# A two-block decoder on one core: the output norm's broadcast in four 32-row tiles over four banks, the output product and its norm in other banks

## The chip, the cores and the metric

The kernel runs on one core of a Trainium2 chip. The metric is the device time of one execution in microseconds (us); where several runs are compared, their median.

## The reference

The input x is 32 sequences of 128 tokens by 128 channels, with a context of 128 tokens by 96 channels for each. Six sublayers follow one another, each as `x = layernorm(x + sublayer(x))`: in block 0 a gated recurrent and self-attention sublayer, a cross attention, and a quantised two-layer network; in block 1 a gated delta-rule attention, a cross attention with a mask on the queries, and a two-layer network followed by a spike count. The change lies in block 1, at the end of the delta-rule attention and the start of the cross attention:

```
O   = delta rule of 16 heads, 64 channels each, over 128 tokens
O   = O * rsqrt(mean over the head's channels of O^2 + eps) * rms_w
O   = O * g                                   # one gate for each head and token
x1  = layernorm(x + O @ Wo.T + bo)
k,v = ctx @ Wkv.T                             # of the cross attention that follows
q   = x1 @ Wq.T
```

The reciprocal root and the gate are one number for each head and token. Their product, called f, has to be spread over the 64 channels of its head before O is multiplied by it.

## The kernel before, in words

Everything is fp32 but for the quantised network, the biases and the masks. Activations lie with channels on the 128 partitions and tokens along the row. Work goes in three loops: block 0 up to its cross attention, a short loop that finds the largest hidden value for the quantisation, and a third loop, from line 979 on, for the quantised network and block 1. In the third loop two sequences are in flight, called lanes 0 and 1, for 16 rounds: 32 passes of one sequence. Each lane has half of PSUM, four banks of 512 fp32 columns each (`b[0]` to `b[3]`), and its own buffers.

The order of work is written by hand. `CSTAGES` lists the stages of a pass; `CSLOTS` holds for each engine a string of zeros and ones that says whose lane's next stage comes next on it, and each engine issues its instructions in just that order. Engines wait for each other by counting semaphores: a wait on a named step (`dve_did("ON0")`) holds everything behind it on that engine. On TensorE the strings give around the change: for lane 0 `bc`, `ykv`, then lane 1's `cd` (two transposes, L1187 and L1188), then `Wo1`; for lane 1 `bc`, `ykv`, then lane 0's `lna` (a warming matmul L356 and the centring product L1023), then `Wo1`. On VectorE they give for lane 0 `bc`, lane 1's `Mm` (L1562), `ykv`; for lane 1 `bc`, `ykv`. `keep_warm` (L352) issues matmuls whose result nobody reads; `CWARM` says how many 128-column units a stage gets, and 0 means none.

The stages that the change touches, in order:

- `O` (L1264): O lies in banks 0 and 1. ScalarE takes squares of it and copies it to SBUF as `C` (steps `Oc0`, `Oc1`, L1456).
- `norm1`: TensorE averages the squares by head with column tiles of 32 into bank 2 (L1287); VectorE and ScalarE make `f` (L1598), whose last step on ScalarE comes after `Oc1`.
- `bc` (L1289 to L1295): for each pair p of heads one matmul of `f` with a 0/1 matrix `expand[:, p, :]` gives 128 channels by 128 tokens. The rows of `f` that pair p needs lie in rows 32(p//2) to 32(p//2)+31. Before, each matmul reads 64 rows of the array (pairs 0 to 3 the upper half, 4 to 7 the lower), pairs 0 to 3 go to bank 2 and pairs 4 to 7 to bank 3. VectorE then multiplies, four pairs at a time (L1603): ON0 is `D[0:4] = bank 2 * C[0:4]`, ON1 is `D[4:8] = bank 3 * C[4:8]`.
- `ykv` (L1309 to L1313): keys and values of the cross attention from the context, 128 columns each, into bank 1. It waits for `Oc1` and for step `S` on VectorE. VectorE spreads the keys over the heads with a mask (`Kbd`, L436), ScalarE copies the values (L414).
- `Wo1` (L1296 to L1304): the output product, eight matmuls accumulated into bank 2, with the residual's centring (L1303) between the fourth and the fifth. The first four wait for ON0, the second four for ON1.
- `lng`, `lngv` (L1017 to L1038): square on ScalarE (L1035), mean over channels on TensorE into bank 0 (L1029), reciprocal root on ScalarE (L462, L464), and x1 on VectorE (L1520).
- `yq` (L1317) into bank 0, `qT` on VectorE (L440), and the scores `yS0` (L370), which fill all four banks with four matmuls on 32 rows of the array each.

In the profile an fp32 matmul of this kernel shows as two records, a transpose as one.

Of the kernel before, what the change touches and what calls it, by code (L numbers as in the profile page):

```python
# [19 lines left out]
ALU = mybir.AluOpType  # L20
# [3 lines left out]
P = 128  # L24
# [8 lines left out]
DK = 64  # L33
NP = H // 2
# [116 lines left out]
def decoder(nc, a):  # L151
    with ExitStack() as ctx:
# [792 lines left out]
        with nc.Block() as block:  # L945
# [6 lines left out]
            def _(dve):  # L952
                count = [0]

                def link(ins):
# [34 lines left out]
                   "10011100110011100100010001100000110101"),  # L990
        }, TAILS)
        C_LOADS = 4
        CWARM = {"h": 0, "conv": 2, "alpha": 3, "F": 0, "norm1": 0, "bc": 0, "fc": 4, "pj": 0, "yq": 1, "Wo1": 0,
                 "lna": 1, "lnav": 0, "lngv": 1, "lny": 0, "lnyv": 0, "lnf": 0, "lnfv": 1,
                 "y": {"S": 0, "P": 0, "OT": 0, "AT": 0}}
        halves = ((0, DK), (DK, P))

# [18 lines left out]

        def pe_norm(pe, it, s, t, stage):  # L1017
            n, b = lane[s], lane[s].bank
            keep_warm(b[{"lna": 2, "lnf": 2}.get(stage, 0)], CWARM[stage])
            if stage == "lna":  # L1020
                pe.wait_ge(pc.dve[s], pc.DV.before(it))
                pe.wait_ge(pf.dve[s], pf.DV.upto(it, "x3"))
                mm(b[1][:, 0:P], center[:, :], n.xin[:, :], start=True, stop=True).then_inc(pc.pe[s], pc.PE.step(s, "lnac"))  # L1023
            elif stage == "ln" + t:
                pe.wait_ge(pc.dve[s], pc.DV.upto(it, {"y": "ys", "f": "lx"}[t]))
                mm(b[1][:, 0:P], center[:, :], n.x3[:, :], start=True, stop=True).then_inc(pc.pe[s], pc.PE.step(s, f"ln{t}c"))
            else:
                pe.wait_ge(pc.act[s], pc.AC.upto(it, f"ln{t}sq"))
                mm(b[0][:, 0:P], mean[:, :], n.sq[:, :], start=True, stop=True).then_inc(pc.pe[s], pc.PE.step(s, f"ln{t}v"))  # L1029

        def act_norm(act, it, s, t, stage):
            n, b = lane[s], lane[s].bank
            if stage == "ln" + t:
                act.wait_ge(pc.pe[s], pc.PE.upto(it, "Wo1" if t == "g" else f"ln{t}c"))
                act.activation(n.sq[:, :], b[2 if t == "g" else 1][:, 0:P], ACT.Square).then_inc(pc.act[s], pc.AC.step(s, f"ln{t}sq"))  # L1035
            else:
                act.wait_ge(pc.pe[s], pc.PE.upto(it, f"ln{t}v"))
                ln_exp(act, pc, it, s, f"ln{t}l", f"ln{t}r", eps5)  # L1038

        with nc.Block() as block:  # L1040
            @block.sync
# [43 lines left out]
            def _(pe):  # L1085
                def advance(s, it, stage):
# [202 lines left out]
                    if stage == "bc":  # L1289
                        keep_warm(b[3], CWARM["bc"])  # L1290
                        dve_did("f")
                        for p in (0, 4, 1, 5, 2, 6, 3, 7):
                            rows = slice(DK * (p // 4), DK * (p // 4) + DK)
                            last = mm(pair_out(p, 2), expand[rows, p, :], n.f[rows, :], start=True, stop=True)  # L1294
                        last.then_inc(pc.pe[s], pc.PE.step(s, "bc"))  # L1295
                    if stage == "Wo1":  # L1296
                        keep_warm(b[0], CWARM["Wo1"])
                        for p in range(NP):
                            if p % 4 == 0:
                                dve_did(f"ON{p // 4}")  # L1300
                            last = mm(b[2][:, 0:P], w_o1[:, p, :], n.D[:, p, :], start=(p == 0), stop=(p == NP - 1))  # L1301
                            if p == 3:
                                mm(b[2][:, 0:P], center[:, :], n.x3[:, :], start=False, stop=False)  # L1303
                        last.then_inc(pc.pe[s], pc.PE.step(s, "Wo1"))  # L1304
                    if stage == "lngv":
                        pe_norm(pe, it, s, "g", "lngv")
                    if stage[0] == "y" and stage[1:] in ("kv", *ATTENTION_STAGES):
                        def project():
                            if stage == "ykv":  # L1309
                                act_did("Oc1")  # L1310
                                dve_did("S")
                                mm(b[1][:, 0:P], w_ykv[0:CTX, 0, :], n.ctxT[0:CTX, :], start=True, stop=True)
                                mm(b[1][:, P:2 * P], n.ctxT[0:CTX, :], w_ykv[0:CTX, 1, :], start=True, stop=True).then_inc(pc.pe[s], pc.PE.step(s, "ykv"))  # L1313
                            else:
                                keep_warm(b[3], CWARM["yq"])
                                dve_did("lng")
                                mm(b[0][:, 0:P], w_yq[:, :], n.x1[:, :], start=True, stop=True).then_inc(pc.pe[s], pc.PE.step(s, "yq"))  # L1317
                        pe_attention(pe, pc, it, s, "y", project, False, False, stage, CWARM["y"])
# [151 lines left out]
            def _(dve):  # L1470
                def advance(s, it, stage):
# [42 lines left out]
                    elif stage in ("lnav", "lngv", "lnyv", "lnfv"):  # L1514
# [2 lines left out]
                        if t == "f":  # L1517
                            dve.wait_ge(pc.stored[s], 16 * it + FIRST)
                        out = {"a": x, "g": n.x1[:, :], "y": n.x2[:, :], "f": n.xn[:, :]}[t]
                        then(dve.tensor_tensor(out, b[2 if t == "g" else 1][:, 0:P], n.rstd[:, :], ALU.mult), "ln" + t)  # L1520
                        if t == "g":
                            then(dve.tensor_copy(n.qmask[:, :], n.mask_u8[:, :]), "qmask")
                            dve_did("qmask")
# [49 lines left out]
                    elif stage == "V0":  # L1573
                        for c in range(2):
                            pe_did(f"V{c}")
                            then(dve.tensor_tensor(n.cV[:, c, :, :], b[c][:, :].rearrange("p (a e) -> p a e", e=DK),
                                                   n.cds[:, 2 * c, :].unsqueeze(2).broadcast_to([P, NP, DK]), ALU.mult), f"cV{c}")
                    elif stage[0] == "X":
                        k = int(stage[1:])
                        pe_did(stage)  # L1580
                        new, out = (n.PT1, n.PT0)[k % 2][:, 4:8, :, :], b[3][:, :].rearrange("p (a k t) -> p a k t", a=4, k=2)
                        if k == LEVELS - 2:
                            new, out = new[:, :, 1, :], out[:, :, 1, :]
                        then(dve.tensor_copy(new, out), stage)  # L1584
                    elif stage == "A":
                        pe_did("A")
                        for i in range(2):
                            then(dve.tensor_tensor(n.AT[:, i, :, :, :], b[2 + i][:, :].rearrange("p (c a t) -> p c a t", c=2, a=4),
                                                   mask_at[:, :].unsqueeze(1).unsqueeze(1).broadcast_to([P, 2, 4, DK]), ALU.mult), f"AT{i}")
                    elif stage == "S":  # L1590
                        pe_did("S")
                        then(dve.tensor_tensor(by_bank(n.S), solved(2), by_bank(n.Fp[:, :, DK - 1:DK].broadcast_to([P, NP, DK])), ALU.mult), "S")
                    elif stage == "norm1":
                        then(dve.tensor_scalar(n.x3[:, :], x, b_o1[:, 0:1], None, ALU.add), "xs")
                        pe_did("mo")
                        then(dve.scalar_tensor_tensor(n.zs[:, 0:P], n.t2[:, 0:P], 1e-6, b[2][:, 0:P], ALU.mult, ALU.add), "ve")
                        act_did("oR")
                        then(dve.tensor_tensor(n.f[:, :], n.rk[:, :], n.gb[:, 0:P], ALU.mult), "f")  # L1598
                    elif stage == "bc":
                        pe_did("bc")  # L1600
                        for i in range(2):
                            act_did(f"Oc{i}")
                            then(dve.tensor_tensor(n.D[:, 4 * i:4 * i + 4, :], pairs(2 + i), n.C[:, 4 * i:4 * i + 4, :], ALU.mult), f"ON{i}")  # L1603
                    elif stage == "yAT":
                        pe_did("yAT")
                        then(dve.tensor_tensor(n.x3[:, :], b[2][:, 0:P], n.x1[:, :], ALU.add), "ys")
                    elif stage == "fc":
                        act_did("fr")
                        then(dve.tensor_tensor(n.h[:, :], n.h[:, :], n.h[:, :], ALU.mult), "fr2")
                    elif stage == "pj":  # L1610

                        pe_did("pj")
                        y, total = b[0][:, 0:P], n.OT[:, P:2 * P]
                        then(dve.tensor_scalar(total, y, SPIKE_AT[0], None, ALU.is_gt), "ls1")
                        for i in range(1, 5):
                            dve_did(f"ls{i}")
                            then(dve.scalar_tensor_tensor(total, y, SPIKE_AT[i], total, ALU.is_gt, ALU.add), f"ls{i + 1}")  # L1617
                        dve_did("ls5")
                        then(dve.scalar_tensor_tensor(n.x3[:, :], total, 0.2, n.x2[:, :], ALU.mult, ALU.add), "lx")
# [115 lines left out]
```

## Time and profile before

| | |
|---|---|
| median of 3 runs | 2691.66 us (2690.64 to 2695.48) |
| the profiled execution | 2695.88 us, its span 2694.1 us |
| mean granted TensorE clock | 0.977 of 2.4 GHz |
| TensorE matmul busy | 2387.6 us, 89% of the span |
| VectorE, ScalarE, GpSimd busy | 61%, 61%, 8% |
| the third loop | from about 1036 us to the end; its 32 broadcasts start between 1045.4 and 2658.2 us |

Matmuls are pipelined, and in the profile the end of one is modelled, so two that follow each other overlap; distances between starts are the safer measure. The timeline merges like instructions that follow each other into one row: its start, the time from there to the end of the last, and how many records. The bracket at the end of a row is the idle time of the engine before it, and what ended it. PEld is TensorE's weight load, which runs beside its matmuls. Releasers are inferred from semaphore events.

### The profile page before, as it was taken

To read this page: it belongs to the slowest core of one execution; us is meant where nothing else is said; L and a number is where in the kernel's file an instruction comes from. 1 tells how busy PE (TensorE), PEld (TensorE's weight loads), DVE (VectorE), ACT (ScalarE), POOL (GpSimd) and SP (SyncE) were. 2 spreads that over 40 slices of the span, in tenths; PEclk is the share of its full clock that TensorE was granted. 3 is DMA by queue.
4 is the path that set the end of the run, shared out by engine and by line. 5 is a ranking of instruction groups with operands and counts; after the bars stand their busy time and mean duration, and the time that the engine had idled before them with its cause. 6 is when DMAs were issued, how large, how long until landed. Compare 5 with 4: busy or idle time off the path is not lost.

```text
span 2694.1 us, 92105 instructions
## 1 busy us (share of the span) xinstructions
PE 2387.6 (89%) x40926; PEld 1747.2 (65%) x40930; DVE 1656.2 (61%) x3852; ACT 1635.3 (61%) x3852; POOL 206.0 (8%) x174
## 2 busy tenths in 40 slices
PE   3899998999899658999999899999999998999997
PEld 2666666666666427677677677676676676776765
DVE  3667776777677555665656556556656655565564
ACT  2767676767676425656656656566566565566563
POOL 0000000000000001001101110110010011011100
PEclk8999999999999869999999999999999999999998
DMA  3000000000000010000000000000000000000000
GB/s 107 7 8 7 9 8 8 7 9 8 8 7 9 18 37 6 7 9 7 7 6 6 8 8 6 9 7 7 8 7 7 8 7 7 8 7 7 7 6 4
DMA packets 50792, 29.10 MB, mean 11 GB/s; under 512 B 19808, under 2 KB 48672, under 8 KB 50400
## 3 DMA queue, kind: packets, MB, share of 16 engines
q1 hardware_dynamic: 46080, 21.28, 2.8%
q8 instruction: 323, 5.29, 0.8%
q10 hardware_dynamic: 4320, 1.97, 0.3%
q14 instruction: 69, 0.57, 0.1%
HBM read 17.98 MB, written 5.24 MB: 9 GB/s over the span
## 4 chain that ended last, share of the span: by engine, by line
PE 39%; DVE 12%; ACT 11%; issue 2%; DMA 0%; SPq 0%; DVEq 0%
PE bank L1104 5%; PE bank L1171 2%; PE bank L1301 2%; PE bank L356 2%; PE bank L1134 2%; ACT PT L1356 2%; PE bank L1234 2%; ACT zels L1356 2%; DVE zels L447 2%; DVE h L1617 1%; DVE m L445 1%; PE bank L1220 1%; PE bank L1294 1%; PE bank L1144 1%; PE bank L1203 1%
## 5 line engine op out<-in xcount | busy, mean ns | idle before, releaser
L356 PE MATMUL bank<-w_gate,ident 128*128 128x256 f32 (+3 forms) x960 | 342.7, 439 | 15.6 <-DVE mx L860 14.0
L1014 POOL TENSOR_TENSOR PT<-zels,unit 128x512 f32<-128x512 f32 x160 | 203.4, 1271 | 1470.2 <-ACT zels L1356 1283.2
L421 ACT ACTIVATE zels<-zels 128x512 f32<-128x512 f32 x384 | 234.3, 626 | 92.3 <-DVE zels L447 89.9
L445 DVE TENSOR_REDUCE m<-bank 128x4 f32<-128x512 f32 x384 | 262.1, 683 | 22.5 <-PE bank L375 11.7
L447 DVE TENSOR_TENSOR zels<-bank,m 128x512 f32<-128x512 f32 x384 | 265.6, 692 | 13.3
L1356 ACT ACTIVATE zels<-bank 128x512 f32<-128x512 f32 (+1 forms) x256 | 142.6, 573 | 155.9 <-PE bank L1220 79.6
L387 PE MATMUL bank<-ident,zels 128*128 128x128 f32 x1536 | 218.4, 278 | 11.1 <-ACT zels L421 9.5
L1356 ACT ACTIVATE PT<-bank 128x512 f32<-128x512 f32 x256 | 147.8, 598 | 89.6 <-PE bank L1277 48.7
L424 ACT ACTIVATE PT<-bank 128x512 f32<-128x512 f32 x384 | 199.6, 594 | 1.8 <-PE bank L387 1.8
L387 PEld LDWEIGHTS bank<-ident,zels 128*128 128x128 f32 x1536 | 172.7, 142 | 36.5 <-ACT zels L421 21.6
L356 PEld LDWEIGHTS bank<-w_gate,ident 128*128 128x128 f32 x960 | 147.1, 193 | 54.2 <-issue 26.3
L1220 PE MATMUL bank<-zels 64*64 64x64 f32 x5120 | 154.9, 220 | 4.5 <-issue 4.4
L1356 ACT ACTIVATE W<-bank 128x512 f32<-128x512 f32 x192 | 114.1, 594 | 54.1 <-PE bank L1234 27.2
L1218 PE MATMUL bank<-zels 64*64 64x64 f32 x4096 | 135.6, 223 | 10.5 <-DVE zels L1584 7.1
L1220 PEld LDWEIGHTS bank<-zels 64*64 64x64 f32 x5120 | 133.0, 135 | 9.7 <-issue 5.9
L370 PE MATMUL bank<-Kbd,qT 32*128 32x512 f32 x768 | 110.4, 643 | 30.1 <-DVE qT L440 16.9
L1218 PEld LDWEIGHTS bank<-zels 64*64 64x64 f32 x4096 | 113.6, 134 | 35.9 <-issue 28.1
L393 PE MATMUL bank<-PT,V 128*32 128x128 f32 x3072 | 124.0, 280 | 3.3
L462 ACT ACTIVATE rstd<-bank,eps 128x128 f32<-128x128 f32 x224 | 81.4, 363 | 51.9 <-PE bank L1029 46.6
L1584 DVE COPY zels<-bank 128x512 f32<-128x512 f32 (+1 forms) x160 | 100.9, 631 | 13.5 <-PE bank L1220 11.9
L393 PEld LDWEIGHTS bank<-PT,V 128*32 128x32 f32 x3072 | 70.9, 109 | 43.0 <-ACT PT L424 36.1
L1234 PE MATMUL bank<-W,PT 64*64 64x64 f32 x4096 | 89.7, 223 | 4.7 <-issue 4.0
(293 smaller groups left out, 5043.8 us busy)
## 6 DMA issues: line engine op xcount, KB each, us to landing
ctxT<-in_ctxT_dram SPq DMA_DIRECT2D x64, 48.0 KB, 1.8
x_after_cross_attention<-x SPq DMA_DIRECT2D x32, 64.0 KB, 1.6
h<-x_after_cross_attention SPq DMA_DIRECT2D x8, 256.0 KB, 2.8
xin<-x_after_cross_attention SPq DMA_DIRECT2D x32, 64.0 KB, 1.8
out_dram<-xn SPq DMA_DIRECT2D x32, 64.0 KB, 1.6
x<-in_xT_dram ACTq DMA_DIRECT2D x30, 64.0 KB, 1.8
input_integers<-xq SPq DMA_DIRECT2D x8, 128.0 KB, 2.0
xq<-input_integers SPq DMA_DIRECT2D x32, 32.0 KB, 1.8
```

The source lines that it names most:

```text
L356: mm(bank[:, 0:cols], ident[:, :], w_gate[:, :, :].rearrange("p a b -> p (a b)")[:, 0:cols], start=True, stop=True)
L387: last = xp(b[u][:, j * P:(j + 1) * P], n.zels[:, u, j * P:(j + 1) * P], ident[:, :])
L393: last = mm(b[0][32 * j:32 * j + 32, u * P:(u + 1) * P], n.V[:, HU * u + j, :], n.PT[:, u, j * P:(j + 1) * P], start=True, stop=True)
L421: act.activation(n.zels[:, u, :], n.zels[:, u, :], ACT.Exp, scale=ATT_SCALE).then_inc(ph.act[s], ph.AC.step(s, f"{t}P{u}"))
L424: act.activation(n.PT[:, u, :], b[u][:, :], ACT.Copy).then_inc(ph.act[s], ph.AC.step(s, f"{t}PT{u}"))
L445: dve.tensor_reduce(top, scores, AX_X, ALU.max).then_inc(ph.dve[s], ph.DV.step(s, f"{t}max{u}"))
L447: dve.tensor_tensor(n.zels[:, u, :].rearrange("p (h k) -> p h k", h=HU), scores, top.unsqueeze(2).broadcast_to([P, HU, P]), ALU.subtract). ...
L1014: pool.tensor_tensor(n.TI[:, k % 2, :, :], (n.PT0, n.PT1)[k % 2][:, :, 1, :], unit[:, :].unsqueeze(1).broadcast_to([P, NP, DK]), ALU.add)\
L1218: mm(solve_out(p, dst, 2, 0, P), PT[src, p, 1, :], PT[src, p, 0, :], start=True, stop=True)
L1220: last = mm(solve_out(p, dst, 2, DK, P), PT[src, p, 0, :], PT[src, p, 1, :], start=True, stop=True)
L1234: last = mm(solve_out(p, dst, 0), n.TI[src, k % 2, p, :], W[src, p, :], start=True, stop=True)
L1356: ins = act.activation(out, src, func, **how)
```

## The change

The broadcast's eight matmuls read 32 rows each in place of 64. Pairs 2j and 2j+1 go to bank j, columns 0 to 127 and 128 to 255, in the order of the even pairs and then the odd ones, so that four matmuls in turn use four different row tiles and four different banks. ON0 reads banks 0 and 1 (256 columns of each), ON1 banks 2 and 3. Since ON0 now reads bank 1, `ykv` waits for ON0 in place of `Oc1` and `S`. The output product goes to bank 0 in place of 2, its variance to bank 2 in place of 0, with the warming matmul ahead of it; ScalarE and VectorE read them there. The warming call in `Wo1`, of zero units, is gone.

```diff
-        CWARM = {... "yq": 1, "Wo1": 0, "lna": 1, ...
+        CWARM = {... "yq": 1, "lna": 1, ...
...
-            keep_warm(b[{"lna": 2, "lnf": 2}.get(stage, 0)], CWARM[stage])
+            keep_warm(b[{"lna": 2, "lnf": 2, "lngv": 2}.get(stage, 0)], CWARM[stage])
...
-                mm(b[0][:, 0:P], mean[:, :], n.sq[:, :], start=True, stop=True).then_inc(...)
+                mm(b[2 if t == "g" else 0][:, 0:P], mean[:, :], n.sq[:, :], start=True, stop=True).then_inc(...)
...
-                act.activation(n.sq[:, :], b[2 if t == "g" else 1][:, 0:P], ACT.Square).then_inc(...)
+                act.activation(n.sq[:, :], b[0 if t == "g" else 1][:, 0:P], ACT.Square).then_inc(...)
...
-                ln_exp(act, pc, it, s, f"ln{t}l", f"ln{t}r", eps5)
+                ln_exp(act, pc, it, s, f"ln{t}l", f"ln{t}r", eps5, b[2 if t == "g" else 0])
...
-                        for p in (0, 4, 1, 5, 2, 6, 3, 7):
-                            rows = slice(DK * (p // 4), DK * (p // 4) + DK)
-                            last = mm(pair_out(p, 2), expand[rows, p, :], n.f[rows, :], start=True, stop=True)
+                        for odd in range(2):
+                            for j in range(4):
+                                p, rows = 2 * j + odd, slice(QR * j, QR * (j + 1))
+                                last = mm(b[j][:, odd * P:(odd + 1) * P], expand[rows, p, :], n.f[rows, :], start=True, stop=True)
...
-                        keep_warm(b[0], CWARM["Wo1"])
...
-                            last = mm(b[2][:, 0:P], w_o1[:, p, :], n.D[:, p, :], start=(p == 0), stop=(p == NP - 1))
+                            last = mm(b[0][:, 0:P], w_o1[:, p, :], n.D[:, p, :], start=(p == 0), stop=(p == NP - 1))
                             if p == 3:
-                                mm(b[2][:, 0:P], center[:, :], n.x3[:, :], start=False, stop=False)
+                                mm(b[0][:, 0:P], center[:, :], n.x3[:, :], start=False, stop=False)
...
-                                act_did("Oc1")
-                                dve_did("S")
+                                dve_did("ON0")
...
-                        then(dve.tensor_tensor(out, b[2 if t == "g" else 1][:, 0:P], n.rstd[:, :], ALU.mult), "ln" + t)
+                        then(dve.tensor_tensor(out, b[0 if t == "g" else 1][:, 0:P], n.rstd[:, :], ALU.mult), "ln" + t)
...
-                            then(dve.tensor_tensor(n.D[:, 4 * i:4 * i + 4, :], pairs(2 + i), n.C[:, 4 * i:4 * i + 4, :], ALU.mult), f"ON{i}")
+                            four = slice(4 * i, 4 * i + 4)
+                            then(dve.tensor_tensor(n.D[:, four, :].rearrange("p (j a) t -> p j a t", j=2),
+                                                   n.psum[:, 2 * i:2 * i + 2, 0:2 * P].rearrange("p j (a t) -> p j a t", a=2),
+                                                   n.C[:, four, :].rearrange("p (j a) t -> p j a t", j=2), ALU.mult), f"ON{i}")
```

## Rows read from the trace of the kernel before

**Rows 1.** The page, busy time of each engine and its share of the span

```profile
PE 2387.6 (89%) x40926; PEld 1747.2 (65%) x40930; DVE 1656.2 (61%) x3852; ACT 1635.3 (61%) x3852; POOL 206.0 (8%) x174
```

**Rows 2.** The page, the chain that ended last, shares by engine

```profile
PE 39%; DVE 12%; ACT 11%; issue 2%; DMA 0%; SPq 0%; DVEq 0%
```

**Rows 3.** Two stretches: length, busy by engine, then granted clock, DMA share, GB/s

```profile
1397.60:1407.80 10.20, 9.93 (x70) 8.62 (x65) 2.96 (x7) 3.95 (x11) 0.00 (x0) 0.50 0.03 8
1410.00:2200.00 790.00, 734.60 (x16159) 556.16 (x16159) 473.35 (x1136) 490.42 (x1132) 95.34 (x75) 1.00 0.03 7
```

**Rows 4.** Timeline of TensorE around a broadcast of lane 0

```profile
1991.36 1.16 PE L1294 MATMUL bank<-f,expand 64*128 64x128 f32 x16
1992.45 0.49 PE L1312 MATMUL bank<-ctxT,w_ykv 96*128 96x128 f32 x2
...
1993.11 0.27 PE L1188 MATMUL bank<-ident,ccdd 128*128 128x128 f32 x1
1993.31 1.16 PE L1301 MATMUL bank<-zels,w_o 128*128 128x128 f32 x8
```

**Rows 5.** Timeline of VectorE in the same stretch

```profile
1991.49 0.29 DVE L1568 TENSOR_TENSOR ccdd<-ccdd,rk 128x128 f32<-128x128 f32 x1
1992.57 1.29 DVE L1603 TENSOR_TENSOR zels<-bank,zels 128x512 f32<-128x512 f32 x2 [0.78 <-PE bank L1294]
```

**Rows 6.** Timeline of TensorE around a broadcast of lane 1

```profile
1925.03 1.16 PE L1294 MATMUL bank<-f,expand 64*128 64x128 f32 x16 [0.43 <-DVE f L1598]
1926.12 0.49 PE L1312 MATMUL bank<-ctxT,w_ykv 96*128 96x128 f32 x2
...
1926.89 0.39 PE L1023 MATMUL bank<-xin,center 128*128 128x128 f32 x2
1927.12 1.06 PE L1301 MATMUL bank<-zels,w_o 128*128 128x128 f32 x8
...
1932.85 0.71 PE L370 MATMUL bank<-Kbd,qT 32*128 32x512 f32 x4 [1.09 <-DVE qT L440]
```

**Rows 7.** Timeline of VectorE in the same stretch

```profile
1925.38 0.29 DVE L1520 TENSOR_TENSOR xn<-bank,rstd 128x128 f32<-128x128 f32 x1 [0.20 <-ACT rstd L464]
1926.24 1.29 DVE L1603 TENSOR_TENSOR zels<-bank,zels 128x512 f32<-128x512 f32 x2 [0.57 <-PE bank L1294]
...
1930.92 0.29 DVE L1520 TENSOR_TENSOR x<-bank,rstd 128x128 f32<-128x128 f32 x1 [0.34 <-ACT rstd L464]
...
1931.38 0.86 DVE L1502 TENSOR_SCALAR h<-xpad,conv_w,conv_b 128x128 f32<-128x128 f32 x3
```

**Rows 8.** Timeline of TensorE and its weight load in the last pass

```profile
2658.19 1.16 PE L1294 MATMUL bank<-f,expand 64*128 64x128 f32 x16 [0.43 <-DVE f L1598]
...
2660.14 0.19 PEld L1301 LDWEIGHTS bank<-zels,w_o 128*128 128x128 f32 x1 [0.34 <-DVE zels L1603]
2660.15 0.38 PE L1301 MATMUL bank<-zels,w_o 128*128 128x128 f32 x1 [0.15 <-DVE zels L1603]
```

**Rows 9.** Timeline of TensorE, two lines that use four tiles of the array

```profile
1999.56 1.14 PE L370 MATMUL bank<-Kbd,qT 32*128 32x512 f32 x8
...
1922.96 0.64 PE L1287 MATMUL bank<-PT,hmean 128*32 128x128 f32 x16 [0.29 <-ACT PT L1356]
```

**Rows 10.** Groups by line and form, VectorE: busy us, mean ns, idle before

```profile
L1603 DVE TENSOR_TENSOR zels<-bank,zels 128x512 f32<-128x512 f32 x64 | 41.2, 686 | 22.3 <-PE bank L1294 22.3
...
L1592 DVE TENSOR_TENSOR S<-bank,Kbd 128x512 f32<-128x512 f32 x32 | 22.0, 688 | 43.4 <-PE bank L1262 43.4
```

**Rows 11.** Line L1603: who waited for it (us in total, times)

```profile
  PEld bank L1301: 3.1, 17
```

**Rows 12.** Timeline of TensorE ahead of the lower clock, and of a late stall

```profile
1395.58 0.35 PE L1277 MATMUL bank<-Qz,S 64*64 64x64 f32 x5 [0.80 <-DVE S L1592]
1396.87 1.18 PE L1277 MATMUL bank<-Qz,S 64*64 64x64 f32 x27 [0.94 <-issue]
...
2287.51 0.33 PE L1238 MATMUL bank<-ident,Km 64*64 64x64 f32 x3 [1.61 <-issue]
```

More of the change, by code:

```diff
@@ L992, in decoder @@
         C_LOADS = 4
-        CWARM = {"h": 0, "conv": 2, "alpha": 3, "F": 0, "norm1": 0, "bc": 0, "fc": 4, "pj": 0, "yq": 1, "Wo1": 0,
-                 "lna": 1, "lnav": 0, "lngv": 1, "lny": 0, "lnyv": 0, "lnf": 0, "lnfv": 1,
+        CWARM = {"h": 0, "conv": 2, "alpha": 3, "F": 0, "norm1": 0, "bc": 0, "fc": 4, "pj": 0, "yq": 1, "lna": 1, "lnav": 0, "lngv": 1, "lny": 0, "lnyv": 0, "lnf": 0, "lnfv": 1,
                  "y": {"S": 0, "P": 0, "OT": 0, "AT": 0}}
@@ L1028, in pe_norm @@
                 pe.wait_ge(pc.act[s], pc.AC.upto(it, f"ln{t}sq"))
-                mm(b[0][:, 0:P], mean[:, :], n.sq[:, :], start=True, stop=True).then_inc(pc.pe[s], pc.PE.step(s, f"ln{t}v"))
+                mm(b[2 if t == "g" else 0][:, 0:P], mean[:, :], n.sq[:, :], start=True, stop=True).then_inc(pc.pe[s], pc.PE.step(s, f"ln{t}v"))
         def act_norm(act, it, s, t, stage):
@@ L1034, in act_norm @@
                 act.wait_ge(pc.pe[s], pc.PE.upto(it, "Wo1" if t == "g" else f"ln{t}c"))
-                act.activation(n.sq[:, :], b[2 if t == "g" else 1][:, 0:P], ACT.Square).then_inc(pc.act[s], pc.AC.step(s, f"ln{t}sq"))
+                act.activation(n.sq[:, :], b[0 if t == "g" else 1][:, 0:P], ACT.Square).then_inc(pc.act[s], pc.AC.step(s, f"ln{t}sq"))
             else:
                 act.wait_ge(pc.pe[s], pc.PE.upto(it, f"ln{t}v"))
-                ln_exp(act, pc, it, s, f"ln{t}l", f"ln{t}r", eps5)
+                ln_exp(act, pc, it, s, f"ln{t}l", f"ln{t}r", eps5, b[2 if t == "g" else 0])
         with nc.Block() as block:
```

## The prediction

> **What bounds the kernel now.** I read the page's busy times first: TensorE is busy 89% of the span, VectorE and ScalarE 61% each [rows 1]. The chain that ended last gives TensorE the largest engine share, 39% against 12% and 11% [rows 2]. In the third loop, which the change touches, a steady stretch of 790 us has TensorE busy 734.6 us, 93%, and VectorE 473.4 us, 60% [rows 3]. So a lane's broadcast stage is worth what it does to the order of work on TensorE, and I read the timeline of that one stage on both engines, once for lane 0 and once for lane 1; all 32 passes repeat these two patterns, but for the last one [rows 8] and one that falls in a stretch at the lower clock [rows 3].
>
> Lane 0 [rows 4, 5]: the broadcast starts at 1991.36 and takes 1.16 us. TensorE then goes straight on with the key and value products ("ykv", L1312 and L1313, 1992.45) and the other lane's two transposes, while VectorE makes the product ON0 from 1992.57. Each of its two products takes 0.69 us [rows 10], so ON0 ends at 1993.26 and the output product (L1301) starts at 1993.31, 0.05 later: it waits for ON0. That wait costs little, because 0.75 us of VectorE's work lies beside TensorE work that was queued behind the broadcast. Lane 1 [rows 6, 7]: the same, but two whole matmuls (a warming one, and L1023) lie in between where lane 0 has two transposes of one record each, so L1301 follows without a wait at 1927.12. In all, L1301 waited for ON0 in 17 passes, 3.1 us together [rows 11]: the 16 of lane 0 and the last of lane 1.
>
> **The change, part by part.** Times are counted from the start of the broadcast.
>
> *Broadcast itself.* Eight fp32 matmuls, 16 records, now take 1.16 us [rows 4], as long as four matmuls on the whole array (L1301, 8 records, 1.16): two run at a time. One beat of the array is (1.16 - 0.49) / 6 = 0.11 us, from L1301's 8 records and L1312's 2 [rows 4]. The stretch of eight beats becomes four, if four row tiles run at a time: 0.49 + 2 x 0.11 = 0.71, with the stagger of four starts 0.72 us. The trace before does not show this very form. Its nearest rows: L370, four 32-row tiles into the four banks, 512 columns each, 8 records in 1.14 us (one after the other they would be 8 records x 4 x 0.11 = 3.5 us); and L1287, 16 records on four column tiles of 32, 0.64 us [rows 9]. The bounds are 0.64 (like L1287) and 1.16 (no gain); I take 0.72, since L370 has the change's tile and banks. The gain on the array is 0.44 us a pass, 14 us over 32 passes, if nothing else changed.
>
> *The new wait.* The broadcast now also fills bank 1, so ykv, next in TensorE's order, must wait for ON0, which reads banks 0 and 1. ykv stood there as the cover. Queued behind it are, in lane 0, the other lane's transposes and L1301; in lane 1, the warming matmul, the other lane's centring (L1023) and L1301. After: broadcast ends at 0.72; ON0 starts 0.05 later as before (1992.57 against 1991.36 + 1.16), at 0.77; VectorE is free by then (0.42 in lane 0: L1568 ends at 1991.78; 0.64 in lane 1: L1520 ends at 1925.67); ON0 ends at 1.46, ykv starts at 1.51. Before it started at 1.09. So ykv is **0.42 us later**: an idle time of 0.79 (0.05 + 0.69 + 0.05) more than eats the 0.44 saved; before, ykv even started 0.07 ahead of the broadcast's end.
>
> *Lane 0, 16 passes.* From ykv's start to the next free beat behind the two transposes is 1993.11 - 1992.45 + 0.11 = 0.77, so L1301 starts at 2.28 instead of 1.95, 0.33 later. It no longer waits, so its first weight load is hidden: its first half takes 1.06 as in lane 1, not 1.16 [rows 4, 6]. Net 0.33 - 0.10 = 0.23 us.
>
> *Lane 1, 15 passes.* Nothing waited there before, so the whole 0.42 us passes on to L1301.
>
> *The last pass.* Nothing of the other lane lies in between [rows 8]: ykv at 1.51, L1301 behind its four beats and the 0.10 of its first load at 2.06 instead of 1.96 (2660.15 - 2658.19), less the 0.10 of L1301's own load, now hidden: 0.
>
> *Does the delay reach the end?* Behind L1301 come the square on ScalarE, the variance product, the two activations of ScalarE, the normalised x1 on VectorE, the query product, and the scores (L370). In lane 1 L370 waits 1.09 us for VectorE's qT [rows 6, 7]. But the work that keeps VectorE busy there (L1502's taps, which start behind x1) is itself started through L1301, so this idle time absorbs nothing. In lane 0 TensorE runs on without a gap. I let all of it through.
>
> *The rest.* VectorE's products read 256 columns of two banks instead of 512 of one: L1592, a 512-element read over two banks, takes 0.69 like L1603 [rows 10]; 0. Output product, square and variance in other banks: same instructions and sizes, no new wait; 0, covered by nothing because there is nothing to cover. ykv has one wait less, on work long done; 0. The warming call of zero units issued nothing. VectorE's second product and the key mask (L436) come 0.44 and some 0.3 us earlier; their reader on ScalarE is not on TensorE's path; 0. No DMA, and no step of SP or POOL, is moved.
>
> A weight load of ykv issued ahead of its wait would soften it. I count none: in the last pass L1301's load starts at 2660.14 and its matmul at 2660.15, both behind ON0 [rows 8].
>
> **Sum:** 16 x 0.23 + 15 x 0.42 + 0 = 3.7 + 6.3 = **+10.0 us**. The profiled execution took 2695.88 us, so it would give 2705.9. It lies 4.2 above the median of the three runs, 2691.66 (2690.64 to 2695.48); on the median the sum gives **2701.7 us**. A difference under 0.2%, 5.4 us, is about what a measurement of this kernel cannot tell from none.
>
> **The rivals.**
> *Absorbed* (0.10): the 1.09 us idle before L370 in lane 1 takes up lane 1's delay, and only lane 0's 3.7 us are left: 2695.4. For it: the idle time is real and follows within 6 us. Against it: what ends it starts behind the delayed product.
> *Faster* (0.06): the end is set through VectorE, by broadcast, ON0, ON1 and what follows them, and not by TensorE's order. Then every pass gains 0.44 x 32 = 14.1: 2677.6. For it: VectorE stood idle before ON0 in every pass, waiting for the broadcast (0.78 and 0.57 in rows 5 and 7), and L1301 did wait for ON0 in 17 passes [rows 11]. Against it: that wait was 0.2 us each. It decides from the point where TensorE has over 0.42 us to spare behind ykv; rows 4 and 6 show none.
> *The tiles don't run four at a time* (0.05), because the 16 weight loads go one after the other: the broadcast stays at 1.16, ykv starts at 1.95, 0.86 late; lane 0 0.77 - 0.10 = 0.67, lane 1 0.86, the last pass 0.34: 10.7 + 12.9 + 0.3 = +24: 2715.6. L370 speaks against it.
> *The load is hidden* (0.04): ykv's first weight load is done while its matmul still waits for ON0. Then 0.10 us less in 31 passes, 10.0 - 3.1 = 6.9: 2698.6. Against it: load and matmul of L1301 started together behind the same wait [rows 8]. The Trainium skill ("TensorE: Matmul & The Clock Gate", "Architectural detail") speaks for it: TensorE's queue can pull weight loads ahead of matmuls in flight.
> *The clock* (one more fall 0.06, one fewer 0.05): in the stretch 1397.6 to 1407.8 the granted clock was 0.50, the lower level of 1.2 GHz, after TensorE had stood idle for 0.80 and for 0.94 us within two [rows 12]; the 790 us after it stood at 1.00 [rows 3]. Such a stretch costs at most half of its 10.2 us. The new wait adds 0.79 us of idle time to every pass, so one more is possible: 10.0 + 5.1, 2706.8. The stalls that end in "issue", as that of 0.94 us and the 1.61 us before L1238 [rows 12], may move with the program, and the one fall may go: 2696.6. The Trainium skill (same page, "What's actually happening") has the clock follow how busy the array has recently been, which is why idle time added in every round is a case of its own here.
>
> **How the numbers follow.** The forecast has 0.64; its own range is 2698 to 2706, from 0.64 for the broadcast (0.08 x 31, 2.5 less) and the spread of the runs (1.0 below the median, 3.8 above). The range from 2692 to 2709 takes in the absorbed case, the hidden load and both of the clock; it leaves out the faster one and the one without four at a time, and the edges of the rest. Slower by over 0.2%: the forecast less 0.02 at its low edge, the hidden load, the 0.05 without four at a time and the 0.06 of one fall more: 0.77. Within 0.2%: absorbed, one fall fewer and the 0.02: 0.17. Faster: 0.06.
>
> **What would show it.** In the changed profile: the broadcast in about 0.72 us; TensorE idle some 0.7 us before ykv, released by VectorE's product; TensorE's busy time about 14 us less over the loop and yet the span longer; L1301 without a wait in both lanes; a lane's pair of rounds some 0.65 us longer. The forecast is wrong if the broadcast stays over 1 us, if ykv's idle time is under 0.4 us, or if L370's idle time shrinks by what ykv's grew.

## The result, and the profile after

The changed kernel takes 2713.35 us, the median of 6 runs (2708.00 to 2720.96), against 2692.28 for the kernel before, also 6 runs: 1.007 of it, with a 95% interval of 1.0055 to 1.0085, so slower by 18.8 us (14.8 to 22.9; the two medians by themselves are 21.1 apart). The forecast was 2701.7, 10.0 more than before, and the range ended at 2709. The side was right; about half of the size was missed.

The page of the changed kernel, busy time and chain by engine, answers to [rows 1, 2]; it moved by nothing that one could read a cause from:

```profile
PE 2387.3 (88%) x40926; PEld 1745.2 (64%) x40930; DVE 1657.0 (61%) x3852; ACT 1636.9 (60%) x3852; POOL 206.2 (8%) x174
...
PE 39%; DVE 12%; ACT 10%; issue 2%; DMA 0%; SPq 0%; DVEq 0%
```

The timeline of TensorE in the changed kernel, around a broadcast of lane 0, answers to [rows 4] (the lines of the code have moved: L1310 is ykv's first product, L1300 the output product, L1022 the centring):

```profile
2005.33 0.73 PE L1294 MATMUL bank<-f,expand 32*128 32x128 f32 x16
2006.87 0.49 PE L1310 MATMUL bank<-ctxT,w_ykv 96*128 96x128 f32 x2 [0.81 <-DVE zels L1602]
2007.20 0.39 PE L1311 MATMUL bank<-w_ykv,ctxT 96*128 96x128 f32 x2
2007.42 0.28 PE L1186 MATMUL bank<-ident,ccdd 128*128 128x128 f32 x1
2007.54 0.27 PE L1187 MATMUL bank<-ident,ccdd 128*128 128x128 f32 x1
2007.64 1.06 PE L1300 MATMUL bank<-zels,w_o 128*128 128x128 f32 x8
```

and around one of lane 1, to [rows 6]:

```profile
1938.57 0.73 PE L1294 MATMUL bank<-f,expand 32*128 32x128 f32 x16 [0.43 <-DVE f L1596]
1940.11 0.49 PE L1310 MATMUL bank<-ctxT,w_ykv 96*128 96x128 f32 x2 [0.81 <-DVE zels L1602]
...
1941.11 1.06 PE L1300 MATMUL bank<-zels,w_o 128*128 128x128 f32 x8
...
1942.22 1.06 PE L1300 MATMUL bank<-zels,w_o 128*128 128x128 f32 x8
...
1946.84 1.14 PE L370 MATMUL bank<-Kbd,qT 32*128 32x512 f32 x8 [1.09 <-DVE qT L440]
```

The timeline of VectorE beside the first of them answers to [rows 5]:

```profile
2006.13 1.29 DVE L1602 TENSOR_TENSOR zels<-bank,zels 128x512 f32<-128x512 f32 x2 [0.37 <-PE bank L1294]
2007.33 0.68 DVE L1560 TENSOR_TENSOR S<-bank,mask_l 128x512 f32<-128x512 f32 x1
```

and in the last pass, to [rows 8]:

```profile
2685.53 0.73 PE L1294 MATMUL bank<-f,expand 32*128 32x128 f32 x16 [0.42 <-DVE f L1596]
...
2687.62 1.06 PE L1300 MATMUL bank<-zels,w_o 128*128 128x128 f32 x8
```

The broadcast takes 0.73 us instead of 1.16: four tiles do run at a time. TensorE then stands idle for 0.81 us, and ykv starts 1.54 us after the broadcast's start instead of 1.09. Counted from the same start, the output product begins at 2.31 instead of 1.95 in lane 0, of which its first weight load, now hidden, gives back 0.10, and at 2.54 instead of 2.09 in lane 1. L370's idle time is 1.09 us as before: it absorbed nothing. In the last pass the output product starts at 2.09 instead of 1.96, less 0.10. So the waits cost 16 x 0.26 + 15 x 0.45 + 0.03 = **10.9 us**, where the forecast had 10.0. A whole round (from one broadcast of lane 0 to the next, one pass of each lane) shows the same: the shortest took 103.8 us before (1679.86 to 1783.69) and 104.5 in the changed kernel (1796.30 to 1900.82), 0.7 more, as 0.26 + 0.45.

The rest shows in another view. Line L1602 of the changed kernel, VectorE's product: who waited for it; below, the stretches between the loop's first and last broadcast in which the granted clock was 0.50, with columns as in [rows 3]:

```profile
  PEld bank L1310: 32.2, 32
  PE bank L1310: 26.0, 32
```

```profile
1302.96:1306.37 3.41, 3.41 (x18) 3.41 (x18) 0.69 (x1) 0.45 (x2) 0.00 (x0) 0.50 0.00 0
1511.18:1521.41 10.23, 9.04 (x62) 8.03 (x63) 3.05 (x7) 2.95 (x10) 0.00 (x0) 0.50 0.03 8
1599.93:1603.33 3.40, 3.40 (x73) 2.99 (x72) 0.69 (x1) 1.63 (x4) 0.06 (x1) 0.50 0.02 5
1729.63:1733.03 3.40, 3.40 (x17) 3.40 (x18) 1.05 (x2) 0.45 (x2) 0.00 (x0) 0.50 0.07 19
2200.67:2207.49 6.82, 6.82 (x92) 4.05 (x96) 1.64 (x5) 3.67 (x7) 0.00 (x0) 0.50 0.00 0
2262.11:2265.52 3.41, 3.41 (x19) 3.41 (x18) 0.69 (x1) 0.45 (x2) 0.00 (x0) 0.50 0.00 0
2364.51:2367.92 3.41, 3.41 (x40) 2.62 (x37) 0.29 (x1) 2.65 (x6) 0.00 (x0) 0.50 0.02 5
2661.47:2664.88 3.41, 3.41 (x55) 2.96 (x59) 0.72 (x2) 2.24 (x4) 0.83 (x1) 0.50 0.02 5
```

Eight stretches, 37.5 us in all, at the lower level of 1.2 GHz. In the kernel before there was one there, of 10.2 us [rows 3]. (Behind the last broadcast the clock fell in both kernels.) Three of the eight, of 3.4 us each, begin 0.2 to 0.7 us after ykv's start in a pass of lane 1, behind the new idle time. The timeline of TensorE at one of them:

```profile
1727.91 0.73 PE L1294 MATMUL bank<-f,expand 32*128 32x128 f32 x16 [0.42 <-DVE f L1596]
1729.45 0.65 PE L1310 MATMUL bank<-ctxT,w_ykv 96*128 96x128 f32 x2 [0.81 <-DVE zels L1602]
...
1731.18 1.91 PE L1300 MATMUL bank<-zels,w_o 128*128 128x128 f32 x8
...
1733.19 1.06 PE L1300 MATMUL bank<-zels,w_o 128*128 128x128 f32 x8
```

From the broadcast to the second half of the output product are 5.28 us; in the undisturbed pass above it is 3.65 (1942.22 - 1938.57). This stretch costs 1.6 us, half of its length.

The other five, 27.3 us in all, begin 13.9 us or more after the ykv before them, with none of the new waits in between: four behind one stall of 1.3 to 1.9 us that ends in "issue" (a stall for which the profile shows no releaser), the fifth behind a wait of 0.79 us for VectorE and a stall of 0.62. The rows ahead of three of them:

```profile
1598.83 0.33 PE L1233 MATMUL bank<-W,PT 64*64 64x64 f32 x5 [1.32 <-issue]
...
2199.07 0.33 PE L1237 MATMUL bank<-ident,Km 64*64 64x64 f32 x4 [1.89 <-issue]
...
2363.44 0.33 PE L1268 MATMUL bank<-Kbd,cV 64*64 64x64 f32 x2 [1.51 <-issue]
```

Such stalls are not new: summed over the rows of TensorE's waits between 1047 and 2650 us they make 21.0 us before and 22.2 in the changed kernel, and the one of 1.61 us in [rows 12] was not followed by a fall. So the stalls themselves carry about 1 us of the difference; whether the new idle time made a fall behind them likelier, no run settles. The profiled executions differ between the first and the last broadcast of the loop by 1636.8 - 1612.8 = 24.0 us; the waits give 10.9 of it, and half of the additional 27.3 us at half clock gives up to 13.6: up to 24.5 in all. This execution was the slowest of the six of the changed kernel, 25.1 us above the profiled one of before, so it shows more of the lower clock than the median run had.

### The profile page after: what moved, and what is told of

It reads as the page before. It is cut to its first block, busy times and chain, and to the rows that moved or that the text cites. A ratio compares the mean times of both kernels' runs of the same rounds, so it can differ in the third digit from the quotient of the medians.

```text
span 2719.2 us, 92073 instructions
## 1 busy us (share of the span) xinstructions
PE 2387.3 (88%) x40926; PEld 1745.2 (64%) x40930; DVE 1657.0 (61%) x3852; ACT 1636.9 (60%) x3852; POOL 206.2 (8%) x174
## 4 chain that ended last, share of the span: by engine, by line
PE 39%; DVE 12%; ACT 10%; issue 2%; DMA 0%; SPq 0%; DVEq 0%
PE bank L1103 5%; PE bank L1170 2%; PE bank L1300 2%; PE bank L1133 2%; PE bank L356 2%; ACT PT L1354 2%; PE bank L1233 2%; ACT zels L1354 2%; DVE zels L447 1%; PE bank L1219 1%; DVE m L445 1%; DVE h L1618 1%; PE bank L387 1%; PE bank L1143 1%; ACT zels L1374 1%
## 5 line engine op out<-in xcount | busy, mean ns | idle before, releaser
L356 PE MATMUL bank<-w_gate,ident 128*128 128x256 f32 (+3 forms) x960 | 343.4, 440 | 15.6 <-DVE mx L860 12.8
L1217 PE MATMUL bank<-zels 64*64 64x64 f32 x4096 | 138.0, 225 | 10.9 <-DVE zels L1582 7.0
L370 PE MATMUL bank<-Kbd,qT 32*128 32x512 f32 x768 | 110.4, 643 | 30.1 <-DVE qT L440 16.9
L1582 DVE COPY zels<-bank 128x512 f32<-128x512 f32 (+1 forms) x160 | 100.8, 630 | 18.7 <-PE bank L1219 17.2
```

What stands on the lines that cost most here:

```text
L356: mm(bank[:, 0:cols], ident[:, :], w_gate[:, :, :].rearrange("p a b -> p (a b)")[:, 0:cols], start=True, stop=True)
L1217: mm(solve_out(p, dst, 2, 0, P), PT[src, p, 1, :], PT[src, p, 0, :], start=True, stop=True)
```

## The experiments

The question was what holds the other half. Theory A: ykv's delay costs 10.9 us, and the rest are stretches at the lower clock that the idle time brings on. Its rivals: the new banks, stalls of the instruction supply, or a delay that grows downstream. Each run was timed beside the kernel before; ratios are to that. e1 to e4 ran on one chip, e5 to e8 on another, e9 to e11 on a third; the changed kernel's own six runs belong to none of these batches, so its 1.007 is compared with theirs through the ratios.

**e1_filled.** A warming matmul inside the wait, in unused columns of bank 3; VectorE's second product waits for it. The list of TensorE's steps gets its name, `bw`.

```diff
                         last.then_inc(pc.pe[s], pc.PE.step(s, "bc"))
+                        mm(b[3][:, 2 * P:4 * P], ident[:, :], w_gate[:, 0:2, :].rearrange("p a b -> p (a b)"), start=True, stop=True).then_inc(pc.pe[s], pc.PE.step(s, "bw"))
...
                             act_did(f"Oc{i}")
+                            if i == 1:
+                                pe_did("bw")
```

> The changed kernel with a warming matmul of 256 columns (two units, fp32, into the unused columns 256 to 511 of bank 3) issued between the broadcast and the wait of ykv; VectorE's second product waits for it. By the changed kernel's trace ykv starts 1.54 us after the broadcast's start and TensorE idles some 0.8 us before it, so the four beats (0.55 us) fit in, and ykv's start stays at 1.54. Theory A (about 10.8 us of the loss are ykv's delay behind ON0, the other 10 are stretches at the lower clock that the idle time brings on): the time at half clock in the third loop falls from 34 us to near the 10 us of before, and the time falls to 2703 us, 1.004 of before. Rival (the other 10 us come from instruction stalls, the new banks, or delay that grows downstream): the time stays at 2713.

Measured: 2704.32 us, 1.0038 (1.0024 to 1.0051), 10.5 us above the 2693.79 of before. Its timeline of TensorE, lane 0:

```profile
2108.35 0.73 PE L1294 MATMUL bank<-f,expand 32*128 32x128 f32 x16
2109.01 0.70 PE L1296 MATMUL bank<-w_gate,ident 128*128 128x256 f32 x2
2109.89 0.49 PE L1311 MATMUL bank<-ctxT,w_ykv 96*128 96x128 f32 x2 [0.18 <-DVE zels L1605]
```

ykv still starts 1.54 us after the broadcast, so the delay is all there, and yet the ratio is 0.0032 (8.6 us) below the changed kernel's 1.007, with the intervals apart: the kernel is faster with work in it that computes nothing. Between the first and last broadcast there are two stretches at half clock, 13.7 us together, instead of eight, and neither begins behind the wait. The mean clock of its runs is 0.9770, against 0.9737 for the changed kernel and 0.9768 for before. What is left over the kernel before is about the sum of the waits.

**e2_wait_alone.** The new layout and wait, but 64-row tiles.

```diff
-                            for j in range(4):
-                                p, rows = 2 * j + odd, slice(QR * j, QR * (j + 1))
+                            for j in (0, 2, 1, 3):
+                                p, rows = 2 * j + odd, slice(DK * (j // 2), DK * (j // 2) + DK)
```

> The changed kernel with the broadcast on 64-row tiles again, two at a time, in the new layout of four banks: all of the change but the four tiles at once. The broadcast takes 1.16 us again instead of 0.73. If four tiles at a time are worth what they measure, each pass starts ykv 0.43 us later still: 13.8 us slower than the changed kernel, 2727 us. If the product of VectorE were bound by something else than the broadcast's end, it would stay near 2713.

Measured: 2722.92 us, 1.0111 (1.0096 to 1.0126). Its timeline of TensorE, lane 0:

```profile
2002.10 1.16 PE L1294 MATMUL bank<-f,expand 64*128 64x128 f32 x16
2004.06 0.49 PE L1310 MATMUL bank<-ctxT,w_ykv 96*128 96x128 f32 x2 [0.79 <-DVE zels L1602]
```

ykv starts 1.96 us after the broadcast, 0.42 later than in the changed kernel. So the four tiles are worth 0.42 us a pass, and between the two kernels 1.0111 - 1.007, 11 us (13.8 were expected, 2727 us; the changed kernel's runs stood at a lower clock, 0.9737 in the mean against 0.9756 here). The tiles are good; it is the wait that the four banks bring with them that loses. One thing speaks against a simple form of theory A: with the same idle time ahead of ykv (0.79 us) the profiled execution of e2 had one slow stretch between its first and last broadcast, of 6.8 us, behind a stall of 1.33 us.

**e3_banks_alone.** The kernel before with the output product and its centring, the source of the square and of x1, the variance and its warming in the new banks; one of the changed lines:

```diff
-                            last = mm(b[2][:, 0:P], w_o1[:, p, :], n.D[:, p, :], start=(p == 0), stop=(p == NP - 1))
+                            last = mm(b[0][:, 0:P], w_o1[:, p, :], n.D[:, p, :], start=(p == 0), stop=(p == NP - 1))
```

> The kernel before with the output product in bank 0 and its variance and warming in bank 2, nothing else. Theory A: no difference, 2692 us within 3. Rival (the new banks, or the code moved by a few instructions, carry the 10 us that the sum missed): 2700 or more.

Measured: 2692.46 us, 0.9998 (0.9985 to 1.0011). No difference: the interval allows 4 us down and 3 up, not the 8 that are looked for. (The broadcast's own four banks are not part of this run.)

**e4_behind.** The changed kernel with ykv issued behind the output product, at the turn of `lng` on TensorE, of `Wo1` on VectorE, and after `lngv` on ScalarE; the names in the lists of steps move too. TensorE's part:

```diff
+                    if stage == "ykv":
+                        return
+                    if stage == "lng":
+                        stage = "ykv"
```

> The changed kernel with ykv issued behind the output product instead of ahead of it (VectorE's Kbd and ScalarE's copy of the values move accordingly). The wait for ON0 is then met by the output product, which had it anyway: it starts 1.54 us after the broadcast's start in place of 2.31 (lane 0) and 2.54 (lane 1), and ykv's four beats come after it, beside ScalarE's square. Net against the kernel before by beats: -0.42 + 0.45 in lane 0, -0.45 + 0.45 in lane 1, so about 2692. TensorE still idles some 0.55 us (lane 0) and 0.2 us (lane 1) behind the broadcast. Theory A: 2692 to 2697, by how often the clock falls. Rival (the loss lies in the layout, not in what is queued behind the wait): 2705 or more.

Measured: 2690.71 us, 0.9992 (0.998 to 1.0003), no difference from the kernel before. Timeline of TensorE, lane 0:

```profile
1881.76 0.73 PE L1294 MATMUL bank<-f,expand 32*128 32x128 f32 x16
...
1883.30 1.16 PE L1300 MATMUL bank<-zels,w_o 128*128 128x128 f32 x8 [0.45 <-DVE zels L1608]
```

The same tiles and the same four banks cost nothing once the work behind the wait is work that had to wait for ON0 anyway.

**e5_reordered.** The changed kernel with two pairs of TensorE's turns exchanged: lane 0's broadcast ahead of lane 1's M, and lane 0's `lna` ahead of lane 1's ykv.

```diff
-            "pe": (35, "100101001010001101011011010111010101000110010000101101110101110011101010110100110101",
-                   "10101011001100101010010101100100011000"),
+            "pe": (35, "100101001010001101010111010111010101000110010000101101110101110011101010110100110101",
+                   "10101010101100101010010101100100011000"),
```

> The changed kernel with two pairs of turns exchanged in TensorE's hand-written order: lane 0's broadcast goes ahead of lane 1's M (0.64 us of TensorE work), so M lies between the broadcast and ykv; and lane 0's lna (four beats) goes ahead of lane 1's ykv. The layout, the tiles and ykv's wait for ON0 are those of the changed kernel. Theory A (the loss is that nothing was left to do behind the broadcast): lane 0's broadcast starts when f is ready, some 0.4 us earlier, and ykv 1.54 us after it, as early as in the kernel before; lane 1 starts the output product 2.09 us after the broadcast, as before. Sum -2 us against before, about 2691 us (2688 to 2695), and the clock falls as seldom as before. Rival (the loss lies in the four banks or the wait itself): 2705 or more.

Measured: 2692.48 us, 0.9988 (0.9973 to 1.0003). Timeline of TensorE, lane 0:

```profile
2090.68 0.73 PE L1294 MATMUL bank<-f,expand 32*128 32x128 f32 x16 [0.17 <-DVE f L1596]
2091.34 0.69 PE L1182 MATMUL bank<-Km,Kp 64*64 64x64 f32 x32
2092.22 0.49 PE L1310 MATMUL bank<-ctxT,w_ykv 96*128 96x128 f32 x2 [0.19 <-DVE zels L1602]
```

M fills the wait, and the loss is gone with ykv's wait still in place. Its 3.9 us below its own before are not clear of zero. Since tiles, banks and wait are all kept, this is the plainest sign that the loss is the idle time: what came of it, delay and clock, went with it.

**e6_behind_nowarm, e7_behind_M_warm, e8_behind_M.** Three kernels on from e4: without the warming ahead of the norm's variance (`"lngv": 0`), with lane 0's broadcast ahead of M, and with both.

> The kernel with ykv behind the output product, and without the warming matmul ahead of the norm's variance (0.22 us of TensorE in each pass). In lane 0 TensorE runs on without a gap there, so 16 x 0.22 = 3.5 us are gained; in lane 1 ScalarE's order (the other lane's root first) holds the chain, so nothing is. 2687 us if the clock holds; if the warming was what kept the clock up, 2692 or more, with more stretches at half clock.

> ykv behind the output product, and lane 0's broadcast ahead of lane 1's M in TensorE's order, so that M covers the wait for ON0. Against the kernel with ykv behind alone (2690.7): lane 0's broadcast starts some 0.4 us earlier, TensorE does not idle before the output product, whose first load is hidden: 0.4 to 0.5 us in 16 passes, 6 to 8 us: 2683 us (2680 to 2687). If the idle time in lane 0 was covered work of another engine all the same, no change: 2691.

> Both together: ykv behind the output product, M behind lane 0's broadcast, no warming ahead of the norm's variance. By beats 3.5 us below the one with the warming, 2680 us; if the clock falls more often without it, 2683 to 2690.

Measured: e6 2697.17 us, 1.0002 (0.9984 to 1.0019); e7 2686.53 us, **0.9953** (0.9937 to 0.9968), faster than both kernels; e8 2695.21 us, 0.999 (0.9975 to 1.0006). Timeline of TensorE in e7, lane 0, with no idle stretch behind the broadcast:

```profile
2090.38 0.73 PE L1294 MATMUL bank<-f,expand 32*128 32x128 f32 x16 [0.17 <-DVE f L1602]
2091.04 0.69 PE L1182 MATMUL bank<-Km,Kp 64*64 64x64 f32 x32
...
2091.83 0.27 PE L1187 MATMUL bank<-ident,ccdd 128*128 128x128 f32 x1
2091.94 1.14 PE L1300 MATMUL bank<-zels,w_o 128*128 128x128 f32 x8
```

Span and mean granted clock of the profiled execution of e8, and of that of e7:

```profile
core 0: 2697.5 us, clock 0.971
```

```profile
core 0: 2689.2 us, clock 0.977
```

Dropping 0.22 us of warming from each pass takes 7 us of work off TensorE. It made e8 8.7 us slower than e7, on one chip and with intervals apart; e6 is no faster than e4 (1.0002 against 0.9992, intervals overlapping). Between first and last broadcast of the profiled executions e6 had six stretches at half clock, 34.1 us, and e8 five, 41.0 us, against one of 6.8 us in e4 and two of 13.7 together in e7. The mean clock over all twelve runs of each says the same without leaning on one execution: 0.9718 in e8 against 0.9776 in e7, 0.9740 in e6. So the expectation that the clock would hold failed; its other branch came, in e8 with a median of 2695.2 above the 2683 to 2690 written there, beside a before that was itself 4 us slower than in the first batches.

**e9_changed_again, e10_filled_half, e11_filled_again.** The changed kernel, and it with one and with two warming units, on one chip.

> The changed kernel itself once more, to have it on one chip beside the two filled ones, with more runs. Theory A: 1.007 of before again, mean granted clock 0.003 lower than the filled kernel's, and 7 to 10 us slower than it. Rival (the gap between the changed and the filled kernel came from the sessions): the three lie within 3 us.

> The changed kernel with one warming unit of 128 columns in the wait instead of two: some 0.4 us of idle time is left in it. Theory A: the mean granted clock and the time lie between the changed and the filled kernel, or at the filled one's if half of the filling is enough: 2703 to 2709 us. Rival: any matmul there changes nothing, 2713.

> The kernel with two warming units in the wait once more, beside the other two on one chip. Theory A: 1.004 of before, 10.8 us, with the clock of the kernel before. Rival: as slow as the changed kernel.

Measured beside a before of 2698.65 us: changed 2715.38, 1.006 (1.0042 to 1.0078); one unit 2709.42, 1.0052 (1.0033 to 1.007); two units 2709.47, 1.0042 (1.0027 to 1.0058). The gap between changed and fully filled is 5.9 us, the side that theory A gives (7 to 10 were expected, under 3 for the rival), but the intervals overlap, and the mean clocks don't carry it: 0.9758 changed, 0.9752 with one unit, 0.9772 with two, 0.9764 before. One unit was expected to lie between the other two in the clock; it lies below both, and yet it is as fast as two. By itself this batch does not settle the question. What it gave is an execution of the changed kernel that hardly fell: the profiled one of e9 took 2703.37 us. Its busy time on the page, its span and mean clock, and its first and last broadcast in the timeline:

```profile
PE 2368.6 (88%) x40926; PEld 1728.9 (64%) x40930; DVE 1657.5 (61%) x3852; ACT 1635.6 (61%) x3852; POOL 206.0 (8%) x174
```

```profile
core 0: 2701.6 us, clock 0.980
```

```profile
1046.03 0.73 PE L1294 MATMUL bank<-f,expand 32*128 32x128 f32 x16
...
2667.95 0.73 PE L1294 MATMUL bank<-f,expand 32*128 32x128 f32 x16 [0.42 <-DVE f L1596]
```

From first to last 1621.9 us, 9.1 more than in the kernel before, with two stretches of 3.4 us at half clock instead of 10.2: the waits' 10.9 less half of 3.4 is 9.2. One of the two begins behind the new wait, the other behind a stall of 1.55 us. That the sum comes out so closely is in part luck: in the profiled execution of e11, with none of the lower clock between first and last broadcast, they are 1625.6 us apart, 12.8 more than before, where the same sum gives 10.9 - 5.1 = 5.8. So 7 us of it are neither waits nor clock; its stalls that end in "issue" make 24.8 us where those of e9 make 19.9. The changed program in its two profiled executions differs by 17.6 us, and TensorE's busy time, with equal records, by 18.7 (2387.3 against 2368.6): slower matmuls, not more idle time, make that difference. Over the 12 unfilled runs, those at a mean clock of 0.977 or more took 2703 to 2708 us, those at 0.975 or less 2712 to 2721.

## Why the prediction was right or wrong

**What bounds the kernel, and the broadcast itself:** right. 0.73 us against 0.72; e2 shows the tiles' share alone.

**The new wait:** right in place and nearly in size. ykv 0.45 later, not 0.42: ON0 started 0.07 after the broadcast's modelled end instead of 0.05, and the broadcast took 0.01 more. Lane 0 cost 0.26 (0.23 forecast), lane 1 0.45 (0.42), the last pass 0.03 (0): 10.9 us for 10.0.

**The delay reaches the end:** right. L370's idle time stayed at 1.09. **The banks, the two-bank reads, ykv's missing wait:** put at 0; e3 shows it for the banks within 4 us, and L1602's 0.69 us a product for the reads. The missing wait was not tried by itself.

**The rivals.** *Absorbed* and *faster* did not occur, nor did *tiles not four at a time*, nor *the load is hidden*: ykv's load waited like its matmul. *The clock* is where the forecast failed. The step that failed is the term of the sum for it: nothing, with one more fall as a rival of 0.06 at up to 5.1 us. The prediction itself had the idle time grow by 0.79 us in every pass, and still priced one event instead of asking how often, in 32 passes, the clock would fall. The runs showed eight stretches and 37.5 us in one execution, two and 6.8 us in another. By the mean clocks, 0.9737 over the changed kernel's six runs against 0.9768 for 25 runs of before in the next batch, some 17 us more were spent at half clock, worth up to 8.4. With the waits that makes up to 19.3 us, against the 18.8 measured; 8.4 is a ceiling. A lower estimate comes from the scatter: over all 180 runs whose clock is on record, runs of one kernel in one batch are 1.75 us longer for each 0.001 of mean clock (least squares), which makes 5.4 us of the clock and leaves 2.5 unexplained, less than the interval of the measurement. The Trainium skill ("TensorE: Matmul & The Clock Gate", "What's actually happening") says that the clock follows how busy the array has recently been. e8 agrees, with fill taken away (0.9718 against e7's 0.9776), and so does e1, with fill that computes nothing (0.9770 against 0.9737, in another batch).

**The busy time** on the page was to fall by 14 us and did not (2387.3): at half clock it grew back. In e9, at a higher clock than before, it fell by 19.0.

**What stays open.** How much of the 18.8 us the clock holds: 5.4 by the slope, up to 8.4 by the ceiling. In the last batch it can hold less: there the changed kernel's mean clock was 0.9758 against 0.9764, at most 1.4 us, and with the waits that is 12.3 of 16.2 us measured (11.3 to 21.0). Compared at like clocks the changed kernel of that batch is still 1 to 3 us over the filled ones; with six runs each that is within the scatter. And it is not shown that the new idle time brought on the five slow stretches that begin elsewhere. Behind the new wait itself the clock fell in four of 64 passes in the two profiled executions of the changed kernel, once in 32 with one unit of fill, and in none of 64 with two. Why at those and not at the next was not tried.

## What to carry to other kernels

A faster form that spreads its output over more banks also claims the bank of the work queued next; count what was hidden behind the old form, and move something else behind the new wait before judging it (e7 gains 0.5% with the very tiles that lost 0.7%). Where TensorE is kept warm by hand, a recurring idle stretch can have a second price in the clock, up to half of each slow stretch that it brings on. Count such stretches in more than one execution, look at what stood idle just ahead of each, and compare the mean granted clock of all runs before explaining a difference under 1%; dropping a warming matmul can cost more than it saves.

## What the runs showed of the hardware

Four fp32 matmuls on 32-row tiles with 128 columns each, into four banks, run side by side: 16 records in 0.73 us, where two at a time on 64-row tiles took 1.16 (e2 has the same four banks and still 1.16).

Idle stretches of only 0.81 us, with others of 0.29 and 0.42 us in the 4 us before them, were followed by 3.4 us at 1.2 GHz in four of the 32 passes of lane 1 in two executions of the changed kernel, and not in the other 28. With 0.45 us of fp32 warming in each of them the time was 8.6 us lower by one comparison across batches (1.007 to 1.0038) and 5.9 by another within one, where the intervals overlap. I had not expected filling to pay without shortening any wait.

The weight load of ykv did not run ahead of its wait: in all 32 passes load and matmul started together, 0.05 us after the end of VectorE's product.
